# A two-layer block on one core: the second normalisation of three batches, the gate columns and the selection move

## The chip, the cores and the metric

The kernel runs on one core of a Trainium2 chip. The metric is the device time of the whole program in microseconds (us). The kernel before takes 1383.87 us, the median of three runs (1381.85 to 1384.41).

## The reference

Four batches of 512 tokens with 128 features (2048 tokens, 16 tiles of 128). Two layers, and each normalises its input and adds two results to it.

```python
xn = _layernorm(x)
x = x + _L0_attn_ref(xn, ...) + _L0_ffn_ref(xn, ...)      # 8 heads of 64; experts: 8, the best one, 80 places each
xn = _layernorm(x)
x = x + _L1_attn_ref(xn, ...) + _L1_ffn_ref(xn, ...)
# in _L1_attn_ref
q, k = xn @ Wq.T, xn @ Wk.T                               # 64 columns each
Vy = xn @ Wy_w.T + Wy_b                                   # 128 columns
e = relu(signed_sqrt(q[:, :, None, :] + k[:, None, :, :]))
scores = einsum('bija,a->bij', e, Wphi)                   # softmax over j, combined with Vy and e
# in _L1_ffn_ref
logits = xn @ gate_w + gate_b                             # 8 experts
topv, topi = top_k(logits, 2); probs = softmax(topv)      # two experts, their shares
```

## The kernel before

Four stages follow each other, each in a block of its own. A block ends for all engines together: the next one starts only when every engine has finished. Inside a block each engine runs its own list of instructions in the order written, and the lists meet at semaphores.

1. `normalise_and_route` loads the tokens into `g.x1`, normalises them into `g.xn`, transposes them into `g.xnT` and finds each token's expert, its slot and its factor `g.coef`.
2. `first_layer` is the attention of layer 0, and inside its first batch the experts of layer 0. A batch (called a row in the code) is 32 steps: 8 heads times 4 tiles of queries. In step s TensorE makes the scores of tile s, VectorE their largest value (L582), ScalarE the exponentials (L512), GpSimd divides by the sum (L462, `rescale`), TensorE transposes the result (L702), ScalarE keeps its rounded part (L525, `pT_hi`), VectorE the rest (L592, `pT_lo`), and TensorE multiplies with the values (L728 to L730). The last operations lag by up to ten steps. Once in four steps the next head's queries and keys are kept (L497, L501 on ScalarE, L564, L569 on VectorE), and in eight steps of each batch the values (L533, L607). The sum over the heads of batch b is copied, transposed and added to `g.x1` in steps 7 to 9 of batch b+1 (L612, L738, L618). After the last batch there is a drain of ten steps, in which only the lagging operations and this last addition are left. GpSimd gathers the experts' results into `g.gathered` during the second batch.
3. `second_route`, the seam between the layers. VectorE adds `g.gathered` times `g.coef` to `g.x1` tile by tile (L843, 16 instructions), takes mean and variance (L91, L94), and ScalarE the square root (L823). VectorE normalises into `xn` (L848), TensorE transposes (L894), ScalarE keeps `g.xnT` (L826). Then TensorE makes the gate logits of all 16 tiles (L901), and after them for each batch c the queries (L910), the keys (L913) and the values (L918), each into one PSUM bank; ScalarE keeps queries and keys (L831, L834), VectorE the values with their bias (L853, `keep_values`). VectorE selects the two experts of each token with `first_max` (five operations, each waiting for the one before) twice (L871, L875), ScalarE takes one exponential of the gap (L837) between batch 1 and batch 2 of its copies, and six small operations make `g.share`.
4. `second_layer` is layer 1: features, square roots and weighted sums of 32 blocks of queries, with one expert's products beside each block. It takes about 1000 of the 1381 us and is not touched by the diff.

Of the kernel before, what the change touches and what calls it, by code (L numbers as in the profile page):

```python
# [100 lines left out]
def layers_kernel(nc, x, wqk, wv, gate0_w, gate0_b, w1, b1, w2, b2,  # L101
# [7 lines left out]
    with ExitStack() as ctx:  # L109
# [25 lines left out]
        g.wq, g.wk, g.wy, g.wyb = (g.wge[:, i * P:(i + 1) * P] for i in range(4))  # L135
# [10 lines left out]
        with ExitStack() as first:  # L146
# [42 lines left out]
            g.gateb = scratch("gateb", [P, E])  # L189

# [154 lines left out]
def first_layer(nc, g, take):  # L345
# [12 lines left out]
    with ExitStack() as ctx:  # L358
# [40 lines left out]
        eo_out, gathered_in = sem("eo_out"), sem("gathered_in")  # L399
        small_in, c2_made, c2_prep = sem("small_in"), sem("c2_made"), sem("c2_prep")  # L400
# [13 lines left out]
        SCATTERS_FIRST, CONSTANTS_AT, GATHERS_AT = 3, 16, 2  # L414

# [10 lines left out]
        def _(sp):  # L426
# [5 lines left out]
            small = ((g.wq, g.a_wq), (g.wk, g.a_wk), (g.wy, g.a_wy), (g.wyb, g.a_wyb.partition_broadcast(P)),  # L432
# [11 lines left out]
        def _(pool):  # L444
# [19 lines left out]

            pool.wait_ge(zeroed, 1)
# [11 lines left out]
            pool.wait_ge(gathered_in, 16 * NT)  # L477

        @block.scalar
        def _(act):  # L480
# [22 lines left out]
            def row(b, first=False, drain=False, final=False):  # L503
                for s in range(DRAIN if drain else STEPS):
# [40 lines left out]
        def _(dve):  # L545
# [25 lines left out]

            def row(b, first=False, drain=False, final=False):
                for s in range(DRAIN if drain else STEPS):
# [29 lines left out]
                    if not drain and s - 1 in VALUES_AT:  # L603
# [4 lines left out]
                                          V_hi[:, j // 2, at].bitcast(F32), ALU.subtract).then_inc(v_kept, 1)  # L608
                    if not first and s == OUT_AT:
# [5 lines left out]
                    if not first and s == OUT_AT + 2:  # L615
                        dve.wait_ge(o_done, b)
                        xr = g.x1[:, bass.ds((b - 1) * TB, TB), :]
# [10 lines left out]
        def _(pe):  # L628
# [44 lines left out]
            def row(b, first=False, drain=False, final=False):  # L673
                for s in range(DRAIN if drain else STEPS):
# [40 lines left out]
                    for m in range(TB):  # L715
# [15 lines left out]
                        if m == TB - 1:  # L731
                            ins.then_inc(av_done, 1)
                    if not first and s == OUT_AT + 1:
# [5 lines left out]
                        ins.then_inc(o_done, 1)  # L739
                    if first:  # L740
                        experts(s)

# [43 lines left out]
def second_route(nc, g, take):  # L786


    with ExitStack() as ctx:  # L789
        def sb(name, shape, dt=F32):  # L790
            return ctx.enter_context(nc.sbuf_tensor(name, shape, dt))

# [3 lines left out]
        xn = take(NT, D)  # L796
        gw = take(E)
        p1 = take(NT)
        p2 = take(NT)
        top2 = take(NT)  # L800
        term = take(NT, E)
        psX = ctx.enter_context(nc.psum_tensor("psX1", [P, 4, 512], F32))
        psL = ctx.enter_context(nc.psum_tensor("psL1", [P, NT, E], F32))
        psP = ctx.enter_context(nc.psum_tensor("psP1", [P, 3, 512], F32))
        gate_in, r_steps = sem("gate1_in"), sem("r_steps")
        var_ready, std_ready = sem("var1_ready"), sem("std1_ready")
        xn_ready, xT_done, xT_kept = sem("xn1_ready"), sem("xT1_done"), sem("xT1_kept")
        logits_done, gap_ready, exp_done = sem("logits1_done"), sem("gap_ready"), sem("exp1_done")
# [3 lines left out]
        bias_steps = sem("bias_steps")  # L812
        block = ctx.enter_context(nc.Block())

        @block.sync
        def _(sp):
            sp.dma_start(gw, g.gate1_w).then_inc(gate_in, 16)
            sp.dma_start(g.gateb[:], g.gate1_b.partition_broadcast(P)).then_inc(gate_in, 16)

        @block.scalar  # L820
        def _(act):
            act.wait_ge(var_ready, 1)
            act.activation(g.std[:], g.std[:], ACT.Sqrt).then_inc(std_ready, 1)  # L823
            for c in range(4):
                act.wait_ge(xT_done, c + 1)
                act.activation(g.xnT[:, c * 512:(c + 1) * 512], psX[:, c, :], ACT.Copy).then_inc(xT_kept, 1)  # L826
# [13 lines left out]
        def _(dve):  # L840
            chain = Chain(dve, r_steps)
            for t in range(NT):
                chain.step(dve.scalar_tensor_tensor(g.x1[:, t, :], g.gathered[:, t, :], g.coef[:, t:t + 1],  # L843
                                                    g.x1[:, t, :], ALU.mult, ALU.add))
            chain.done()
            norm_scale(dve, chain, g.x1, g.stats, g.mv, g.std[:], g.rstd[:], var_ready, std_ready)
            for t in range(NT):
                dve.tensor_scalar(xn[:, t, :], g.x1[:, t, :], g.mv[:, t, 0:1], g.rstd[:, t:t + 1],  # L848
                                  ALU.subtract, ALU.mult).then_inc(xn_ready, 1)

            def keep_values(c):
                dve.wait_ge(v_done, c + 1)
                dve.tensor_tensor(g.V2[:, c * TB:(c + 1) * TB, 0:D], psP[:, 2, :].rearrange("p (t d) -> p t d", t=TB),  # L853
                                  g.value_bias.unsqueeze(1).to_broadcast([P, TB, D]), ALU.add).then_inc(v_kept, 1)


            dve.wait_ge(bias_done, 1)
            dve.tensor_tensor(g.value_bias, psP[:, 0, 0:D], g.web, ALU.add).then_inc(bias_steps, 1)
            dve.wait_ge(bias_steps, 1)
            dve.tensor_tensor(g.value_bias, g.value_bias, g.wyb, ALU.add).then_inc(bias_steps, 1)  # L860

# [7 lines left out]
            dve.wait_ge(logits_done, 1)  # L869
            chain.link(dve.tensor_tensor(g.lg[:], psL[:], g.gateb[:].unsqueeze(1).to_broadcast([P, NT, E]), ALU.add))  # L870
# [6 lines left out]
            keep_values(1)  # L877
# [7 lines left out]
            keep_values(2)  # L885
            keep_values(3)

        @block.tensor
        def _(pe):

# [662 lines left out]
```

## Time and profile before

| | |
|---|---|
| median of three runs | 1383.87 us |
| the profiled execution's own time | 1383.03 us |
| its span, first to last instruction | 1381.3 us |
| VectorE, TensorE, ScalarE, GpSimd busy | 88%, 88%, 82%, 64% of the span |
| last batch of the first layer with its drain | about 265 to 344.3 us |
| the seam (`second_route`) | 344.5 to 375.7 us |
| second layer | 375.7 us to the end |
| mean granted TensorE clock | 0.981 of full |

The span is from the first to the last instruction of one profiled execution; the own time has 1.7 us around it. Busy times are shares of the whole, over stages with different limits, so a stage is read by the windows and the list of instructions of its own stretch. A value in square brackets behind an instruction is the idle time of its engine ahead of it, with the instruction that ended it.

### The profile page before, as it was taken

What the parts mean: (1) busy time and instruction counts of PE and PEld (TensorE: products, weight loads), DVE (VectorE), ACT (ScalarE), POOL (GpSimd) and SP (SyncE); (2) the same over time, 40 slices, a digit from 0 to 9 for tenths busy, and PEclk for the clock granted to TensorE, in tenths of its full rate; (3) what the DMA queues carried; (4) which work ended last, traced back from release to release, by engine and by line L of the source; (5) the groups of instructions that cost most, each with busy time, mean ns of one, the idle gap of its engine ahead of it and who ended that gap; (6) DMA issues with size and microseconds to landing.
All of it is one profiled execution on the core that took longest, in us unless ns stands there. A gap on an engine that the chain in (4) does not pass through costs nothing.

```text
span 1381.3 us, 21175 instructions
## 1 busy us (share of the span) xinstructions
PE 1210.2 (88%) x6185; PEld 575.5 (42%) x6185; DVE 1212.5 (88%) x3409; ACT 1135.1 (82%) x1292; POOL 888.8 (64%) x1294
## 2 busy tenths in 40 slices
PE   3899999998659999888999989899988889998886
PEld 2577667676422333333333333333333333333333
DVE  5777989896778899999999999989999998999997
ACT  1776888886369998999999899999989999998950
POOL 0764733332007888888888788888888888888820
PEclk9999999999769999999999999999999999999998
DMA  6001100000000001000000100000000000001001
GB/s 193 9 11 24 30 1 0 0 1 1 20 0 16 20 20 28 23 27 20 20 20 20 32 23 24 20 20 20 20 31 27 20 21 20 20 21 31 28 20 35
DMA packets 38843, 32.36 MB, mean 23 GB/s; under 512 B 6150, under 2 KB 35609, under 8 KB 38738
## 3 DMA queue, kind: packets, MB, share of 16 engines
q1 hardware_dynamic: 37714, 29.76, 7.4%
q0 software_dynamic: 1024, 1.35, 0.6%
q8 instruction: 47, 0.77, 0.2%
q14 instruction: 58, 0.48, 0.1%
HBM read 29.10 MB, written 2.75 MB: 23 GB/s over the span
## 4 chain that ended last, share of the span: by engine, by line
DVE 35%; PE 32%; issue 5%; ACT 1%; POOL 0%; POOLq 0%; DVEq 0%; ACTq 0%
DVE arena L1051 21%; PE ps L1331 10%; PE ps L1344 9%; DVE arena L1037 5%; PE ps L1388 4%; PE ps L1408 4%; DVE s L1083 3%; DVE x L1094 2%; PE ps L1380 2%; PE ps L1362 2%; DVE spread L1103 2%; DVE nmax L1043 1%; PE ps L1366 1%; ACT arena L1190 1%; DVE shift L1045 0%
## 5 line engine op out<-in xcount | busy, mean ns | idle before, releaser
L1051 DVE SCALAR_TENSOR_TENSOR arena<-arena,ps 128x512 f32<-128x512 f32 x1024 | 663.8, 677 | 69.8 <-PE ps L1344 68.5
L1190 ACT ACTIVATE arena<-arena,eps 128x4096 f32<-128x4096 f32 x128 | 474.2, 3709 | 6.0 <-ACT arena L1178 5.7
L1308 POOL TENSOR_SCALAR arena<-kT,negq 128x512 f32<-128x512 f32 x480 | 344.0, 723 | 170.8 <-DVE arena L1051 161.8
L1344 PE MATMUL ps<-spread,sel 128*128 128x512 f16 x1024 | 357.9, 386 | 101.1 <-DVE arena L1051 95.0
L1314 POOL TENSOR_SCALAR arena<-arena,q 128x512 f32<-128x512 f32 x480 | 348.0, 735 | 22.4
L1344 PEld LDWEIGHTS ps<-spread,sel 128*128 128x128 f16 x1024 | 91.9, 97 | 491.5 <-DVE arena L1051 376.0
L1331 PE MATMUL ps<-arena,phi_cols 128*32 128x512 f32 x2048 | 276.3, 614 | 7.7 <-ACT arena L1190 7.7
L1178 ACT ACTIVATE arena<-kT,q 128x512 f32<-128x512 f32 x330 | 217.1, 712 | 44.3 <-DVE arena L1051 44.3
L462 POOL TENSOR_SCALAR kT<-kT,region 128x512 f32<-128x512 f32 x128 | 88.8, 694 | 155.6 <-DVE region L587 155.0
L512 ACT ACTIVATE kT<-ps,region 128x512 f32<-128x512 f32 x128 | 88.0, 687 | 59.4 <-DVE region L582 57.9
L1395 PE MATMUL ps<-z,wge 128*128 128x512 f32 x256 | 130.8, 593 | 0.3 <-DVE z L1077 0.3
L1037 DVE TENSOR_SCALAR arena<-kT,q 128x512 f32<-128x512 f32 x214 | 118.8, 577 | 0.3 <-PEq L789 0.3
L582 DVE TENSOR_REDUCE region<-ps 128x1 f32<-128x512 f32 x128 | 88.1, 689 | 24.8 <-PE ps L687 23.9
L592 DVE TENSOR_TENSOR pT_lo<-ps,pT_hi 128x512 fp32r<-128x512 f32 x128 | 86.9, 679 | 11.2 <-ACT pT_hi L525 10.9
L1331 PEld LDWEIGHTS ps<-arena,phi_cols 128*32 128x32 f32 x2048 | 41.2, 109 | 116.5 <-issue 104.0
L702 PE MATMUL ps<-ident,kT 128*128 128x128 f32 x512 | 77.4, 274 | 9.3 <-DVE pT_lo L592 9.2
L1051 DVE DVE_READ_ACCUMULATOR arena<-arena,ps 128x1 f32 x1024 | 80.2, 78 | 0.0
L702 PEld LDWEIGHTS ps<-ident,kT 128*128 128x128 f32 x512 | 61.3, 140 | 44.8 <-issue 20.1
L525 ACT ACTIVATE pT_hi<-ps 128x512 fp32r<-128x512 f32 x128 | 75.6, 590 | 2.9 <-PE ps L702 2.2
L1380 PE MATMUL ps<-xnT,w1e 128*128 128x512 f32 x128 | 68.2, 615 | 5.0 <-DVE x L1155 5.0
L1408 PEld LDWEIGHTS ps<-w3e,s 128*128 128x128 f32 x512 | 67.8, 193 | 1.6
L1388 PE MATMUL ps<-xnT,w2e 128*128 128x512 f32 x128 | 67.3, 608 | 0.3 <-DVE z L1077 0.3
(196 smaller groups left out, 1714.9 us busy)
## 6 DMA issues: line engine op xcount, KB each, us to landing
wge<-in_e_wg SPq DMA_DIRECT2D x32, 256.0 KB, 2.7
w1e<-in_e_w SPq DMA_DIRECT2D x32, 128.0 KB, 2.1
w2e<-in_e_w SPq DMA_DIRECT2D x32, 128.0 KB, 2.1
w3e<-in_e_w SPq DMA_DIRECT2D x32, 128.0 KB, 2.1
region<-in_w SPq DMA_DIRECT2D x1, 2048.0 KB
out<-x SPq DMA_DIRECT2D x4, 256.0 KB, 2.8
region<-in_wqk SPq DMA_DIRECT2D x1, 512.0 KB, 4.7
region<-in_wv SPq DMA_DIRECT2D x1, 512.0 KB, 5.4
```

Of the source, the lines that this page charges most:

```text
L702: ins = pe.transpose(ps[:, TBK[late % 2], m * P:(m + 1) * P], ex[:, late % 4, m * P:(m + 1) * P], g.ident[:])
L1037: dve.tensor_scalar(feat[:, j, QUADS * gg + c, :], kT[:, bass.ds(b * N, N)], q2[:, bass.ds(pair0 + GROUPS * c + gg, 1)], 0.0, ALU.add, ALU ...
L1051: dve.scalar_tensor_tensor(feat[:, j, k, :], feat[:, j, k, :], 1.0, psB[:, k % BANKS, :], ALU.mult, ALU.mult, accum_out=sums[:, j, gg, c:c ...
L1178: act.activation(feat[:, j, QUADS * gg + c, :], kT[:, bass.ds(b * N, N)], ACT.Relu, bias=q2[:, bass.ds(pair0 + GROUPS * c + gg, 1)]).then_ ...
L1190: act.activation(grp, grp, ACT.Sqrt, bias=eps[:]).then_inc(e_ready, 2)
L1308: pool.tensor_scalar(feat[:, j, QUADS * gg + c, :], kT[:, b * N:(b + 1) * N], HUGE, negq[:, b % 2, at - b * N // 2:at - b * N // 2 + 1], A ...
L1314: pool.tensor_scalar(f, f, 1.0, q2[:, at:at + 1], ALU.mult, ALU.add).then_inc(pool_feat, 1)
L1331: ins = pe.matmul(psS[32 * c:32 * (c + 1), :], phi_cols[:, gg, :], feat[:, j, QUADS * gg + c, :], start=(gg == 0), stop=(gg == GROUPS - 1))
L1344: pe.matmul(psB[:, k % BANKS, :], sel[:, gg, c, :], spread[:, j, :], start=True, stop=True).then_inc(bc_done, 1)
L1388: pe.matmul(psX, w2[:, f * P:(f + 1) * P], xnT[:, bass.ds(m // E * N, N)], start=True, stop=True).then_inc(right_done, 1)
L1395: ins = pe.matmul((psZ, psX)[f], wg[:, half * DFF + f * P:half * DFF + (f + 1) * P], z[:, half, :], start=(half == 0), stop=(half == 1))
L1408: ins = pe.matmul(psY[:, i * D:(i + 1) * D], s[:, f, i * P:(i + 1) * P], w3[:, f * D:(f + 1) * D], start=(f == 0), stop=(f == GT - 1))
```

## The change

- The addition of the experts' results is split. In the last batch GpSimd multiplies `g.gathered` by `g.coef` tile by tile in its first 16 steps (`scale`), and VectorE adds a batch at a time (`mix`) at the end of steps 13, 17, 21 and 25.
- In the same batch VectorE takes mean and variance of the 12 tiles of batches 0 to 2 (`statistics`, steps 19 to 31), and in the drain, after step 4, normalises them into `g.xn` (`normalise`). ScalarE takes their square root in step 3 of the drain. TensorE transposes them (`turn`) around the last output transposes in steps 7 and 8, and ScalarE copies the three results to `g.xnT` in step 9.
- In the seam only the last batch's four tiles are normalised and transposed. The gate's 8 columns stand beside the 128 value columns in one weight tile `g.wyg` (136 columns), loaded during the first layer; the separate logits matmuls are gone. Value products come first (`values`), into four banks, then queries and keys. VectorE keeps logits and values of each half batch, and the whole selection stands after all four batches are kept. ScalarE's list keeps its order: the exponential of the gap still stands behind the copies of batch 1.

```diff
+        MIX_AT = {13: 0, 17: 1, 21: 2, 25: 3}
+        STATS_AT = {19: (0, 1), 20: (2, 3), 23: (4, 5), 24: (6, 7), 27: (8, 9), 28: (10, 11)}
+        AGGR_AT = {20: (0, 1), 23: (2, 3), 24: (4, 5), 27: (6, 7), 28: (8, 9), 31: (10, 11)}
+        SOONER = NT - TB
+        ROOT_AT, NORM_AT = 3, 4
+        SOONER_BANKS = (SB[0], SB[1], PJ)
...
+                pool.tensor_scalar(g.gathered[:, t, :], g.gathered[:, t, :], 1.0, g.coef[:, t:t + 1],
+                                   ALU.mult, ALU.mult).then_inc(scaled, 1)
...
+                    if drain and s == ROOT_AT:
+                        act.wait_ge(var0_ready, 1)
+                        act.activation(g.std[:, 0:SOONER], g.std[:, 0:SOONER], ACT.Sqrt).then_inc(std0_ready, 1)
+                    if drain and s == DRAIN - 1:
+                        for c in range(B - 1):
+                            act.wait_ge(xT0_done, c + 1)
+                            act.activation(g.xnT[:, c * N:(c + 1) * N], ps[:, SOONER_BANKS[c], :],
+                                           ACT.Copy).then_inc(xT0_kept, 1)
...
+            def mix(b):
+                xr = g.x1[:, b * TB:(b + 1) * TB, :]
+                dve.wait_ge(scaled, (b + 1) * TB)
+                dve.tensor_tensor(xr, xr, g.gathered[:, b * TB:(b + 1) * TB, :], ALU.add).then_inc(mixed, 1)
...
+            def normalise():
+                dve.wait_ge(std0_ready, 1)
+                dve.reciprocal(g.rstd[:, 0:SOONER], g.std[:, 0:SOONER]).then_inc(rstd0_ready, 1)
+                dve.wait_ge(rstd0_ready, 1)
+                for t in range(SOONER):
+                    dve.tensor_scalar(g.xn[:, t, :], g.x1[:, t, :], g.mv[:, t, 0:1], g.rstd[:, t:t + 1],
+                                      ALU.subtract, ALU.mult).then_inc(xn0_ready, 1)
...
+                    if drain and s == OUT_AT:
+                        turn(0)
...
+                    if drain and s == OUT_AT + 1:
+                        turn(1)
+                        turn(2)
...
-            for t in range(NT):
-                chain.step(dve.scalar_tensor_tensor(g.x1[:, t, :], g.gathered[:, t, :], g.coef[:, t:t + 1],
-                                                    g.x1[:, t, :], ALU.mult, ALU.add))
+            for t in range(LAST, NT):
+                chain.step(dve.bn_stats(g.stats[:, t, :], g.x1[:, t, :]))
...
+                for half in range(2):
+                    t = c * TB + half * 2
+                    made = psV[:, c % 2, half, 0:2 * (D + E)].rearrange("p (t n) -> p t n", t=2)
+                    dve.tensor_tensor(g.lg[:, t:t + 2, :], made[:, :, D:D + E],
+                                      g.gate1b[:].unsqueeze(1).to_broadcast([P, 2, E]), ALU.add).then_inc(lg_made, 1)
+                    dve.tensor_tensor(g.V2[:, t:t + 2, 0:D], made[:, :, 0:D],
+                                      g.value_bias.unsqueeze(1).to_broadcast([P, 2, D]), ALU.add).then_inc(v_kept, 1)
+
+            keep_values(0)
+            keep_values(1)
...
+            keep_values(2)
+            keep_values(3)
+            dve.wait_ge(lg_made, 2 * B)
             first_max(dve, chain, g.lg[:], g.desc[:], g.top[:], g.tie[:], g.rank[:], g.mask1[:])
-            keep_values(0)
-
             chain.link(dve.scalar_tensor_tensor(g.lg[:], g.mask1[:], -1e30, g.lg[:], ALU.mult, ALU.add))
             first_max(dve, chain, g.lg[:], g.desc[:], top2, g.tie[:], g.rank[:], g.mask2[:])
             dve.tensor_tensor(p2, top2, g.top[:], ALU.subtract).then_inc(gap_ready, 1)
-            keep_values(1)
...
+            values(0)
+            values(1)
+            query(0)
+            for i in range(TB):
+                pe.wait_ge(xn_ready, i + 1)
+                ins = pe.transpose(psX[:, i * P:(i + 1) * P], xn[:, LAST + i, :], g.ident[:])
+            ins.then_inc(xT_done, 1)
+            values(2)
+            pe.wait_ge(xT_kept, 1)
+            values(3)
+            key(0)
+            for c in range(1, B):
+                query(c)
+                key(c)
```

## Rows read from the trace of the kernel before

**Rows 1.** Windows: stretch, length, each engine's busy time, granted clock, DMA.
```profile
265.00:344.50 79.50, 73.88 (x360) 53.37 (x358) 63.72 (x128) 58.77 (x131) 23.36 (x34) 1.00 0.00 1
344.50:375.70 31.20, 20.63 (x98) 14.26 (x99) 21.94 (x96) 10.69 (x20) 0.00 (x0) 0.73 0.01 1
```

**Rows 2.** Windows of four steps each in the last batch, same columns.
```profile
285.62:295.05 9.43, 9.19 (x44) 6.49 (x43) 8.52 (x18) 8.04 (x18) 2.77 (x4) 1.00 0.01 2
303.99:312.15 8.16, 7.78 (x40) 5.57 (x39) 6.88 (x14) 6.52 (x16) 2.77 (x4) 1.00 0.00 1
```

**Rows 3.** Timeline, VectorE in the last batch: start, duration, instruction, idle before.
```profile
306.28 0.69 DVE L582 TENSOR_REDUCE region<-ps 128x1 f32<-128x512 f32 x1 [0.23 <-PE ps L687]
...
307.38 0.69 DVE L592 TENSOR_TENSOR pT_lo<-ps,pT_hi 128x512 fp32r<-128x512 f32 x1 [0.34 <-ACT pT_hi L525]
...
312.15 0.69 DVE L582 TENSOR_REDUCE region<-ps 128x1 f32<-128x512 f32 x1 [0.61 <-PE ps L687]
```

**Rows 4.** Timeline, ScalarE in the same steps.
```profile
307.25 0.68 ACT L512 ACTIVATE kT<-ps,region 128x512 f32<-128x512 f32 x1
...
312.88 0.69 ACT L512 ACTIVATE kT<-ps,region 128x512 f32<-128x512 f32 x1 [0.33 <-DVE region L582]
```

**Rows 5.** Timeline of the drain.
```profile
337.70 0.60 ACT L525 ACTIVATE pT_hi<-ps 128x512 fp32r<-128x512 f32 x1 [1.23 <-PE ps L702]
...
338.33 0.69 DVE L592 TENSOR_TENSOR pT_lo<-ps,pT_hi 128x512 fp32r<-128x512 f32 x1 [1.14 <-ACT pT_hi L525]
...
342.13 0.69 DVE L612 COPY q<-ps 128x512 f32<-128x512 f32 x1 [3.11 <-PE ps L730]
...
343.57 0.69 DVE L618 TENSOR_TENSOR x<-x,ps 128x512 f32<-128x512 f32 x1 [0.75 <-PE ps L738]
```

**Rows 6.** Timeline, VectorE at the start of the seam, like instructions merged.
```profile
344.59 4.29 DVE L843 SCALAR_TENSOR_TENSOR x<-region,coef,x 128x128 f32<-128x128 f32 x16 [0.33 <-PEq L358]
348.92 3.19 DVE L91 BATCH_NORM_STATS2 stats<-x 128x6 f32<-128x128 f32 x16
352.14 1.17 DVE L94 BATCH_NORM_AGGREGATE mv<-stats 128x2 f32<-128x6 f32 x16
...
354.10 4.19 DVE L848 TENSOR_SCALAR region<-x,mv,rstd 128x128 f32<-128x128 f32 x16
```

**Rows 7.** Windows in the seam, for the granted clock (third column from the right).
```profile
362.50:365.00 2.50, 2.50 (x4) 0.96 (x4) 1.72 (x6) 0.69 (x2) 0.00 (x0) 0.50 0.00 0
...
366.00:375.60 9.60, 8.68 (x44) 5.62 (x42) 5.88 (x17) 6.03 (x12) 0.00 (x0) 1.00 0.00 0
```

**Rows 8.** Timeline, TensorE's projections in the seam; two or eight passes merged.
```profile
362.30 1.95 PE L910 MATMUL psP<-xnT,wge 128*128 128x512 f32 x2
...
371.90 1.02 PE L910 MATMUL psP<-xnT,wge 128*128 128x512 f32 x2
...
373.62 1.05 PE L918 MATMUL psP<-wge,xnT 128*128 128x128 f32 x8
```

**Rows 9.** Timeline, second half of the selection, and the table load beside it.
```profile
367.56 0.28 DVE L874 SCALAR_TENSOR_TENSOR lg<-mask,lg 128x128 f32<-128x128 f32 x1
...
369.22 1.28 ACT L837 ACT_TABLE_LOAD   x1
...
369.50 0.17 DVE L876 TENSOR_TENSOR region<-region,top 128x16 f32<-128x16 f32 x1
```

**Rows 10.** Groups of the seam on ScalarE: count, busy, mean ns, idle before.
```profile
L831 ACT ACTIVATE q<-psP 64x256 f32<-64x256 f32 x8 | 3.0, 375 | 7.0 <-PE psP L910 6.9
...
L834 ACT ACTIVATE kT<-psP 128x512 f32<-128x512 f32 x4 | 2.4, 597 | 1.1 <-PE psP L913 0.9
```

**Rows 11.** Timeline, ScalarE at a change of table in the second layer.
```profile
409.37 1.28 ACT L1190 ACT_TABLE_LOAD   x1
410.67 3.71 ACT L1190 ACTIVATE arena<-arena,eps 128x4096 f32<-128x4096 f32 x1
```

**Rows 12.** One line: ns of the shortest, median and longest, two SBUF inputs.
```profile
L1103 DVE SCALAR_TENSOR_TENSOR spread<-exh,split_by,ex x32: 740/741/1197, 414.3 to 1344.7; 128x512 f16<-128x512 f16 x32
```

More of the change, by code:

```diff
@@ L134, in layers_kernel @@
         g.value_bias = g.w1e[:, 0:D]
-        g.wq, g.wk, g.wy, g.wyb = (g.wge[:, i * P:(i + 1) * P] for i in range(4))
+        g.wq, g.wk, g.wyb = (g.wge[:, i * P:(i + 1) * P] for i in range(3))
         g.web, g.rho = g.w3e[:, 0:P], g.w3e[:, P:2 * P]
@@ L476, in _ @@
                         gather(s - GATHERS_AT)
-            pool.wait_ge(gathered_in, 16 * NT)
+                    if b == B - 1 and s < NT:
+                        scale(s)
         @block.scalar
@@ L608, in row @@
                                           V_hi[:, j // 2, at].bitcast(F32), ALU.subtract).then_inc(v_kept, 1)
+                    if final:
+                        statistics(s)
+                    if drain and s == NORM_AT:
+                        normalise()
                     if not first and s == OUT_AT:
@@ L616, in row @@
                         dve.wait_ge(o_done, b)
+                        if drain:
+                            dve.wait_ge(mixed, B)
                         xr = g.x1[:, bass.ds((b - 1) * TB, TB), :]
@@ L822, in _ @@
             act.wait_ge(var_ready, 1)
[L823 to L826, printed above, removed]
+            act.activation(g.std[:, LAST:NT], g.std[:, LAST:NT], ACT.Sqrt).then_inc(std_ready, 1)
+            act.wait_ge(xT_done, 1)
+            act.activation(g.xnT[:, LAST * P:NT * P], psX[:], ACT.Copy).then_inc(xT_kept, 1)
             qv = psP[:, 0, :].rearrange("p (n h) -> p n h", h=2)
@@ L847, in _ @@
-            for t in range(NT):
+            for t in range(LAST, NT):
+                chain.step(dve.bn_aggr(g.mv[:, t, :], g.stats[:, t, :]))
+            chain.done()
+            dve.tensor_scalar(g.std[:, LAST:NT], g.mv[:, LAST:NT, 1], LN_EPS, None, ALU.add).then_inc(var_ready, 1)
+            dve.wait_ge(bias_done, 1)
+            dve.tensor_tensor(g.value_bias, psP[:, 0, 0:D], g.web, ALU.add).then_inc(bias_steps, 1)
+            dve.wait_ge(std_ready, 1)
+            chain.link(dve.reciprocal(g.rstd[:, LAST:NT], g.std[:, LAST:NT]))
@@ L848, in _ @@
+            for t in range(LAST, NT):
                 dve.tensor_scalar(xn[:, t, :], g.x1[:, t, :], g.mv[:, t, 0:1], g.rstd[:, t:t + 1],
                                   ALU.subtract, ALU.mult).then_inc(xn_ready, 1)
+            dve.wait_ge(bias_steps, 1)
+            dve.tensor_tensor(g.value_bias, g.value_bias, g.wyb, ALU.add).then_inc(bias_steps, 1)
             def keep_values(c):
                 dve.wait_ge(v_done, c + 1)
[L853 to L854 removed]
@@ L884, in _, with values, query @@
             dve.tensor_tensor(g.share[:], term, g.mask2[:], ALU.add)
[L885 to L886 removed]
         @block.tensor
         def _(pe):
[L891 to L905 removed]
+            def values(c):
+                if c >= 2:
+                    pe.wait_ge(v_kept, 2 * (c - 1))
+                    pe.wait_ge(lg_made, 2 * (c - 1))
+                for i in range(TB):
+                    t = c * TB + i
+                    ins = pe.matmul(psV[:, c % 2, i // 2, i % 2 * (D + E):(i % 2 + 1) * (D + E)],
+                                    g.xnT[:, t * P:(t + 1) * P], g.wyg[:], start=True, stop=True)
+                ins.then_inc(v_done, 1)
+            def query(c):
                 if c:
```

96 lines of the change are left out of this document (49 added, 47 removed).

## The prediction

> **What bounds the kernel now.** I read the windows first, because the busy shares of the whole say little: VectorE is at 88% over three stages with different limits. The change touches the last batch with its drain and the seam [rows 1]. The second layer starts when the block of the seam has ended for all engines, so every microsecond of the seam counts once; in the seam VectorE is busy for 21.94 of 31.20 us and TensorE for 20.63, one after the other, and the granted clock averages 0.73. The reader should see a serial chain there. The timeline gives its pieces: VectorE alone until 354.1 (mixing 4.29, statistics 3.19 and 1.17, small ones 0.7) while TensorE has nothing to do; then normalising, 4.19 [rows 6]; then the logits and, from 362.30, the projections to 375.4 [rows 8].
>
> The last batch is different. Four steps take 8.16 us, with VectorE at 6.88, ScalarE at 6.52 and TensorE at 7.78 busy [rows 2]. Nobody is full; the three wait for each other in turn, and what VectorE has spare is three small gaps, 0.23, 0.34 and 0.61 us [rows 3].
>
> **The last batch.** VectorE gets 4 mixes, 12 statistics, 12 aggregations and one addition. Like instructions follow each other every 0.20 us (3.19/16) and 0.073 us (1.17/16) [rows 6]; a 128x512 addition lasts 0.69 [rows 5] and takes about 0.60 of the engine, since neighbours overlap by 0.08. That is 2.40 + 2.40 + 0.88 + 0.15 = 5.8 us of work. How much becomes time?
>
> A mix stands behind the kept query, at a place where 0.23 us are idle [rows 3], so it pushes the next maximum by 0.4. That exponential starts at 307.25 with no idle time ahead of it [rows 4]: ScalarE had been busy, and the maximum had ended at 306.97. So the exponential moves by 0.2 and the rest part at 307.38, which waits for ScalarE, not at all. I take 0 for a mix. The nearest measured row is the output addition of the same size at the same place in step 9: its four steps took 9.43 against 8.16 [rows 2], but these also hold two parts of the values and four transposes on TensorE. It is the upper bound.
>
> Two statistics behind step 19 and two with two aggregations behind step 20 put 0.40 + 0.55 us into a stretch that ends in the 0.61 gap at 312.15 [rows 3]. About 0.3 stays over, and there the exponential does wait for the maximum [rows 4], so it is passed on. Three such pairs of steps: 0.9. The last two aggregations and the addition behind step 31 fall ahead of a wait for ScalarE; 0.1 to 0.3. Sum for the batch: +1.2. Bounds: 0, everything in the gaps, and +5.8, nothing.
>
> GpSimd gets 16 scales of 128x128. Its busy time is 2.77 in four steps of 8.16 [rows 2]; a scale is shorter than one of its 0.69 rescales, which are four times as wide, and fits behind each. I take 0; 0 to 0.7 as bounds. Should these scales be late, the mix of step 13 waits for the four of steps 0 to 3, far behind.
>
> **The drain.** Before, ScalarE ends at 338.30, VectorE at 339.02, then VectorE waits 3.11 us for the last product, copies at 342.13 and adds at 343.57, end 344.26 [rows 5]. Into these 3.11 us goes the normalising, but it has to wait for a root. The root's table is not loaded, since the batch uses the exponential: a load of 1.28 and a root that starts right behind it [rows 11], 0.21 for the root. 338.31 + 1.28 + 0.22 = 339.8. Reciprocal 0.25 and its wait, then 12 tiles at 0.262 (4.19/16) [rows 6]: 340.1 + 3.15 = 343.3. The copy comes at 343.3 in place of 342.13, so the addition ends at 345.4. Behind the four output transposes TensorE has eight more, each 0.12 to 0.16 at full clock: 345.8. ScalarE, which copies the three transposed batches last in its list, copies the first at 342.8 and the others at 345.3 and 345.85, 0.60 each, and ends at 346.45. New late one: ScalarE's third copy. The drain grows by 346.45 − 344.26 = 2.2. Bounds: 1.1, if the copies hide (VectorE's end alone), and 3.4, if the clock is at half and the eight transposes take twice as long.
>
> The Trainium skill (*ScalarE: Activation LUTs*, "What ACT_TABLE_LOAD costs") puts a switch at about 2.66 us, load and drain together, against the 1.28 + 0.02 of the row above. By that the root would come 1.4 later, and the sum would be 1.4 worse; the trace disagrees, and the sum goes by the trace.
>
> **The seam, counted from its start.** Gone: the mixing (4.29), three quarters of statistics (2.39 + 0.88) and of normalising (3.14), 12 transposes and 3 copies, and the separate logits, 3.8 us of TensorE. The eight columns beside 128 cost 8/128 of the value products, 0.06 us a batch.
>
> VectorE: 4 statistics 0.80, 4 aggregations 0.30, addition 0.18 and waits: 1.45. Bias 0.28 beside the root; reciprocal and four tiles 2.0 to 3.1; second bias 3.4. TensorE starts values at 0.5 without waiting. After the idle end of the drain I take it at half clock for four to five microseconds: the same projection ran at 0.50 and 1.95 us at 362.5, and at 1.00 and 1.02 us from 366 on [rows 7, 8]. Values of one batch: 0.95 at full (1.05 less overlap [rows 8], plus the columns), 1.9 at half. So values(0) 2.4, values(1) 4.3, first query 5.6, transposes 6.1, values(2) 7.0, values(3) 8.0, first key 8.9. ScalarE's copy of the last transposes is at 6.75, ahead of values(3).
>
> VectorE keeps a batch in about 1.0 (four instructions, between the 0.17 and the 0.69 of their widths): batches 0 and 1 by 5.5, constants 6.1, batches 2 and 3 by 9.15. Now the selection, all behind it. Its second half, from the masking to the gap, is 367.56 to 369.67 = 2.1 [rows 9], the first half five of its steps = 1.6: gap at 12.9. Here the change adds a wait that was not one before: ScalarE's exponential stands behind the copies of batch 1, which end at 11.2. It waits till 12.9, and behind it are queued the query and key copies of batches 2 and 3, and for these TensorE waits, because there is one bank for queries and one for keys. The table load of 1.28 lies in this wait, as it ran ahead of the gap before [rows 9]. From there: exponential 13.15, query copy 0.78 (two of 0.375 and a start [rows 10]), query(3) 1.02 (a copy releases it at 13.95), its copy 15.8, and key copy 0.60: 16.45. VectorE's six small ones end at 14.8. With 0.28 to the next block: 16.7 against 31.14 (344.56 to 375.70), a gain of 14.4. If the clock is full from the start, TensorE is 2 us earlier, VectorE only 0.7: 15.0. Bounds of the seam: 12 to 16.
>
> **The second layer.** The same instructions start earlier, from the same state; its first 40 us go through stretches at either clock, so I allow ±1.5 and take 0.
>
> Sum: +1.2 + 2.2 − 14.4 = −11.0. Against the profiled execution's own 1383.03 that is 1372.0; the median of the runs is 0.84 above that execution, which gives 1372.9. I forecast 1372.5.
>
> The Trainium skill (*SBUF — State Buffer*, "SBUF: two separate sides") says that a VectorE instruction with two SBUF inputs and a GpSimd instruction that reads SBUF exclude each other for their whole length. The mix has two SBUF inputs, and GpSimd rescales all through the batch. Four collisions at 0.69 would make the sum −8.2. The trace shows such a VectorE instruction at 741 ns in the median and 1197 at the longest of 32, with GpSimd busy beside it [rows 12]: a wait exists but is rare.
>
> **Rivals.**
> 1. The batch pays in full, +5.8. For: the loop has no full engine but is a ring of waits, and the additions of step 9 came with longer steps. Against: the gaps [rows 3]. Time 1372.5 + 4.6 = 1377.
> 2. TensorE stays at half clock through the seam. For: projections did run at half for 3.5 us [rows 7] right after the clock had been full. Against: from 366 the same mix ran at full. Then values(3) end at 10.8, gap at 15.6; TensorE's pairs take 1.74 in place of 0.86, and queries and keys of the last two batches stand behind the exponential: end about 23.5, seam gain 7.2. Time 1380.
> 3. Slower than before: the two engines' new instructions exclude each other in the last batch. Place: 16 scales and 4 mixes against maxima, rest parts and rescales there. Price: one full wait of 0.69 for each of the 20, 13.8, on top of 5.8; sum 19.6 + 2.2 − 14.4 = +7.4, 1390. It decides from 12.2 us of growth of the batch. Against it: rows 12, and GpSimd's free 66%.
> 4. The selection hides after all, for ScalarE gets its gap before the copies of batch 1 are done. Then TensorE's pairs bound the seam: 8.0 + 7 × 0.86 + copy 0.7 = 14.7, gain 16.1: 1371. Against: it would need the gap 1.7 us sooner.
> 5. The seam saves, but something gives it all back in the second layer, whose tiles are long (unchanged period): no change, 1383.
>
> **Chances.** Forecast, 1369.5 to 1375.5: 0.68. Rival 1: 0.13. Rival 2: 0.07. Rival 3: 0.02. Rival 4: 0.06. Rival 5: 0.04. A measurement of this kernel tells some 0.2%, 2.8 us, from no change. Faster by over 0.2% are the forecast, rivals 1, 2 and 4: 0.94; within: 0.04; slower: 0.02. The range leaves out rivals 2, 3 and 5 and the thin ends: 1369.3 to 1378.
>
> **What would show it.** The last batch's steps 17 to 29 take 24.5 us before; 25.4 would be right, 28 rival 1. In the drain: a table load at once behind the last rounded part, VectorE's copy near 1.2 us later than the last product, ScalarE's third copy as the last instruction. In the seam: 16.5 us, ScalarE's exponential after an idle of about 0.4 to 1.7 us that VectorE's gap ended, and a TensorE gap ahead of query(3). If instead the seam ends soon after VectorE's keeping, the placing of that wait is wrong; if TensorE's clock is at 0.50 past its fifth microsecond, rival 2 is at work. The forecast is wrong above all if the second layer's start is not 9 to 13 us earlier.

## The result and the profile after

The changed kernel takes 1366.05 us (median of three, 1365.13 to 1366.76) against 1383.87: 0.9882 of before, 95% interval 0.9858 to 0.9905, so 17.8 us faster. The forecast was 1372.5 with a range of 1369.3 to 1378. The direction was right, the forecast gain of 11 us too small, and the time lies outside the range. In a second comparison, that of the run `after_again`, the ratio was 0.9845 (0.9823 to 0.9867).

The profiled execution took 1366.76 us, span 1365.0. Read by stages, the pair of profiles gives this:

| stage | before | after | difference | forecast |
|---|---|---|---|---|
| copy of step 7 to last maximum of the last batch | 49.44 | 49.96 | +0.5 | +1.2 |
| last maximum to the seam's first instruction | 12.24 | 14.11 | +1.9 | +2.2 |
| seam | 31.14 | 14.99 | −16.1 | −14.4 |
| start of the second layer to its first spread | 38.52 | 36.90 | −1.6 | 0 ± 1.5 |
| rest of the second layer | 967.05 | 966.42 | −0.6 | 0 |

With 0.3 us from ahead of step 7 that is −16.3, the two spans.

First the last batch after the change, windows of four steps (columns as in [rows 1]). They answer to [rows 2]:

```profile
303.65:311.93 8.28, 7.88 (x41) 5.56 (x40) 8.16 (x21) 6.39 (x15) 2.78 (x4) 1.00 0.00 1
...
311.93:320.34 8.41, 7.96 (x41) 5.49 (x39) 8.29 (x24) 6.83 (x16) 2.79 (x4) 1.00 0.01 2
```

VectorE is now busy for 8.29 of 8.41 us, where it had 6.88 of 8.16; 1.3 to 1.4 us of work a group became 0.12 to 0.25 us of time. From the maximum of step 17 to that of step 29 it is 25.11 us, before 24.49; the prediction named 25.4 as the sign of its being right and 28 as that of rival 1. One scale on GpSimd takes 0.37 us behind a rescale, with 0.8 to 1.6 us idle ahead of the next rescale.

The drain, from the timeline (start, duration, instruction, idle before), answers to [rows 5]:

```profile
338.55 1.28 ACT L550 ACT_TABLE_LOAD   x1
...
339.84 0.21 ACT L550 ACTIVATE std<-std 128x12 f32<-128x12 f32 x1
...
340.35 3.17 DVE L624 TENSOR_SCALAR region<-x,mv,rstd 128x128 f32<-128x128 f32 x12
...
343.43 0.68 DVE L671 COPY q<-ps 128x512 f32<-128x512 f32 x1
...
344.66 1.04 PE L816 MATMUL ps<-ident,region 128*128 128x128 f32 x8
...
345.30 1.08 ACT L554 ACTIVATE xnT<-ps 128x512 f32<-128x512 f32 x2 [1.90 <-PE ps L816]
```

Each of these instructions starts within 0.25 us of where the forecast put it. The reader should see the root 0.01 us behind its table load: the 2.66 us for a switch that the Trainium skill gives (*ScalarE: Activation LUTs*, "What ACT_TABLE_LOAD costs") are not seen here either.

The seam is one window, all of it at full clock; it answers to the second row of [rows 1], where the mean clock was 0.73:

```profile
346.69:361.67 14.98, 12.48 (x54) 7.12 (x55) 11.83 (x55) 7.49 (x16) 0.00 (x0) 1.00 0.00 1
```

And its end, ScalarE, TensorE and VectorE, answers to [rows 8, 9]:

```profile
356.50 1.28 ACT L905 ACT_TABLE_LOAD   x1
...
357.60 0.17 DVE L955 TENSOR_TENSOR rstd<-region,top 128x16 f32<-128x16 f32 x1
357.81 0.22 ACT L905 ACTIVATE rstd<-rstd 128x16 f32<-128x16 f32 x1
...
358.75 1.12 PE L981 MATMUL psP<-xnT,wge 128*128 128x512 f32 x2 [1.00 <-ACT q L899]
...
360.76 0.60 ACT L902 ACTIVATE kT<-psP 128x512 f32<-128x512 f32 x1
```

The gap (the difference of the two best logits, L955) is ready at 357.77 and the table at 357.78. The queue behind this exponential is as forecast: TensorE waits 1.00 us for the query bank, and the last key copy ends the seam.

### The profile page after: what moved, and what is told of

It reads as the page before. It is cut to its first block, busy times and chain, and to the rows that moved or that the text cites. A ratio compares the mean times of both kernels' runs of the same rounds, so it can differ in the third digit from the quotient of the medians.

```text
span 1365.0 us, 21144 instructions
## 1 busy us (share of the span) xinstructions
PE 1200.5 (88%) x6153; PEld 568.3 (42%) x6153; DVE 1210.0 (89%) x3410; ACT 1135.8 (83%) x1293; POOL 895.9 (66%) x1310
## 4 chain that ended last, share of the span: by engine, by line
DVE 35%; PE 32%; issue 6%; ACT 1%; POOL 0%; POOLq 0%; DVEq 0%; ACTq 0%
DVE arena L1133 22%; PE ps L1413 10%; PE ps L1426 9%; DVE arena L1119 5%; PE ps L1470 4%; PE ps L1490 4%; DVE s L1165 3%; DVE x L1176 2%; PE ps L1462 2%; PE ps L1444 2%; DVE spread L1185 2%; DVE nmax L1125 1%; PE ps L1448 1%; ACT arena L1272 1%; PE ps L1477 0%
```

## The experiments

Stage lengths are read from each run's profile, since the whole varies between executions by more than some of the effects (the kernel before lay between 1379 and 1387 us in all but one of its executions).

**The same kernels again.** What belongs to a kernel, and what to an execution?

> The kernel before, once more, for one profile. From the start of the second layer's block to its first spread it took 39.97 us less 1.45, that is 38.5 (375.73 to 414.25), against 36.9 (361.68 to 398.58) in the changed kernel, and in the changed one TensorE's clock rose earlier there. Theory: the gain in the second layer follows from the change, since TensorE enters it differently; then this profile shows 38.5 again, within 0.3. Rival: where the clock falls and rises there depends on the execution alone; then this profile may lie anywhere from 36.9 to 38.5, and nothing of it is the change's.

> The changed kernel once more, with its time against the kernel before on the same chip. 17 us faster, 1366. Theory (the entry decides): block start to first spread 36.9 again, within 0.3. Rival (each execution has its own): up to 38.5. The seam is 15.0 us in both, since its TensorE work ran at the full clock all through.

> The kernel before, once more for its profile. Theory: in its seam the clock rises at no fixed instruction, and the seam's length follows it: 31.1 to 31.2 us where the clock is full for the logits (as in the first profile), 34.8 where it stays at half through them (as in the second); so the base that I forecast from was the lucky one of two. This one: 31 to 35, and its length follows the time at which the clock rises. Rival: 31.1 is the rule and 34.8 an exception that the median doesn't hold: 31.0 to 31.3.

> The same, a fourth profile. Theory: seam between 31 and 35 us, again following the clock. Rival: 31.0 to 31.3.

| execution | seam | layer start to first spread | rest | time |
|---|---|---|---|---|
| before | 31.14 | 38.52 | 967.05 | 1383.03 |
| before_again | 34.82 | 37.85 | 965.49 | 1384.85 |
| before_third | 35.13 | 37.69 | 965.66 | 1382.03 |
| before_fourth | 32.47 | 37.69 | 965.61 | 1379.04 |
| after | 14.99 | 36.90 | 966.42 | 1366.76 |
| after_again | 14.99 | 38.46 | 967.05 | 1369.23 |

The seam of the kernel before has no fixed length. Its 32 passes of logits show why; the timelines of before_again and of before_fourth:

```profile
358.97 6.83 PE L901 MATMUL psL<-region,xnT 128*128 128x8 f32 x32
...
365.66 2.05 PE L910 MATMUL psP<-xnT,wge 128*128 128x512 f32 x2
```

```profile
355.41 4.27 PE L901 MATMUL psL<-region,xnT 128*128 128x8 f32 x32
...
359.54 2.05 PE L910 MATMUL psP<-xnT,wge 128*128 128x512 f32 x2
```

6.83 us (in before_third too) for what took 3.83 in the profile I forecast from. In before_again the granted clock stayed at 0.50 through all of it:

```profile
361.00:363.00 2.00, 2.00 (x11) 2.00 (x11) 0.00 (x0) 0.00 (x0) 0.00 (x0) 0.50 0.00 0
```

In the profile I forecast from, the clock was full for most of the logits and fell behind them, with TensorE busy throughout (the logits last from 358.6 to 362.4; from 362.5 the clock is at 0.50 [rows 7]):

```profile
360.00:362.00 2.00, 2.00 (x20) 2.00 (x20) 0.00 (x0) 0.00 (x0) 0.00 (x0) 1.00 0.00 0
```

The four seams average 33.4 us, mine was the shortest. Measured against this mean the seam gains 18.4, not 16.1; it is a mean of four executions that differ by 4 us. The start of the second layer is the other way round: after_again took 38.46, as long as any of before, so the 1.6 us there belonged to that execution. My theory that the entry decides is refuted; the rival holds.

The whole time varies for one more reason, which the traces show though no run was made for it. The first stage also makes gate logits, 32 passes of 8 columns. The timelines of before and of before_fourth:

```profile
17.00 6.83 PE L336 MATMUL psL<-gw,xnT 128*128 128x8 f32 x32
```

```profile
16.91 3.74 PE L336 MATMUL psL<-gw,xnT 128*128 128x8 f32 x32
```

They take 6.83 us in 12 of the 16 profiles, and 3.7 to 4.2 in the other four: before_third, before_fourth, move_only and narrow_logits. These four are also the ones that reach the copy of step 7 at 279.6 to 280.1 us, where all others reach it at 282.5 to 283.2. In the four, the granted clock fell about 20 us after the start, in the last part of these passes. In the other twelve the clock column reads 1.00 in this stage, but a pass takes 0.21 us, as at 0.50 in the seam of before_again; there the duration tells, not the column. The pair before and after both had the long one, so their difference of 16.3 us holds nothing of it.

**The two halves of the change, each alone.** `seam_only` leaves the first layer as it was and has only the new order and the joined gate columns; `move_only` has only the moved work, and its seam makes logits, then query, key and value products batch by batch. Both are shown against the changed kernel, shortened:

```diff
 # seam_only: nothing in the last batch or drain; in the seam, for all 16 tiles
-                    if b == B - 1 and s < NT:
-                        scale(s)
...
-                    if final:
-                        statistics(s)
-                    if drain and s == NORM_AT:
-                        normalise()
...
+            for t in range(NT):
+                chain.step(dve.scalar_tensor_tensor(g.x1[:, t, :], g.gathered[:, t, :], g.coef[:, t:t + 1],
+                                                    g.x1[:, t, :], ALU.mult, ALU.add))
...
+            for t in range(NT):
+                if t in (2 * TB, 3 * TB):
+                    pe.wait_ge(xT_kept, t // TB - 1)
+                pe.wait_ge(xn_ready, t + 1)
+                ins = pe.transpose(psX[:, t // TB % 2, (t % TB) * P:(t % TB + 1) * P], xn[:, t, :], g.ident[:])
...
 # move_only: the seam's TensorE list in the old order
+            for t in range(NT):
+                ins = pe.matmul(psL[:, t, :], g.xnT[:, t * P:(t + 1) * P], g.wyg[:, D:D + E], start=True, stop=True)
+            ins.then_inc(logits_done, 1)
+            for c in range(B):
+                xc = g.xnT[:, c * N:(c + 1) * N]
...
```

> Only the second half of the change: nothing is moved into the first layer; in the seam all 16 tiles are mixed, normalised and transposed first, and then come the joined value products, queries, keys and the selection in the new order. Theory: front of the seam as before, 13.8 us to the last normalised tile, then the rest about as long as in the changed kernel, with TensorE at half clock in the first microseconds: seam 27 to 28 us against 31.1, so 3 to 4 us faster than before (1380). Rival, the order and the joined columns carry the larger part of the seam's gain: 24 us, 7 faster.

> Only the first half: mixing, statistics, normalising and transposing of three batches stand in the last batch and the drain as in the changed kernel; the seam makes its logits with separate matmuls and its projections and selection in the old order. Theory: the last batch and drain cost 2.4 us as in the changed kernel; the seam is transposes at about 3.5, logits 1.9 to 3.8, and projections as before 11 to 13: 18 to 19 us; total 10 to 11 us faster than before (1373). Rival (the order carries the larger part): the seam stays at 22 us or more, 7 us faster.

Measured: seam_only 1378.07 us, 0.9956 of before (0.9938 to 0.9975), seam 28.40. move_only 1376.47, 0.9939 (0.9918 to 0.9959), seam 23.49, not the 18 to 19 I expected. The first is near the expectation. The second missed by 5 us: its seam is where the rival had it (22 us or more), and its time is 8.4 us below the 1384.89 of before, between the 10 to 11 of the theory and the 7 of the rival. Its windows show where the 5 us are:

```profile
343.80:347.00 3.20, 1.24 (x6) 0.73 (x7) 2.98 (x16) 0.20 (x1) 0.00 (x0) 1.00 0.01 3
347.00:349.00 2.00, 2.00 (x14) 2.00 (x13) 0.69 (x6) 0.60 (x1) 0.00 (x0) 0.66 0.00 0
349.00:351.00 2.00, 2.00 (x11) 2.00 (x11) 0.00 (x0) 0.00 (x0) 0.00 (x0) 0.50 0.00 0
...
355.00:357.00 2.00, 2.00 (x4) 0.74 (x3) 0.44 (x2) 0.76 (x2) 0.00 (x0) 0.50 0.00 0
```

The seam starts at full clock. The clock falls at about 347.6, 0.5 us after the logits (matmuls of 8 columns) have begun, and stays at half through them and the first projections, about 10 us, with TensorE busy all the time. Ahead of the logits TensorE had been busy for only 1.24 of 3.20 us, so this run alone leaves two causes for the fall, the idle time and the narrow matmuls. Against the mean seam of 33.4 the halves gain 5.0 and 9.9, together 14.9; both at once gain 18.4.

**Is it the narrow matmuls, or the idle time ahead?** Three kernels on the changed one:

```diff
 # narrow_logits (12 matmuls of 8 columns) and wide_logits (12 of 128), results unused
+            for t in range(LAST):
+                pe.matmul(psL[:, t * E:(t + 1) * E], g.xnT[:, t * P:(t + 1) * P], g.wyg[:, D:D + E], start=True, stop=True)
             values(0)
 # the same matmul in wide_logits
+                pe.matmul(psL[:, t % 4 * D:(t % 4 + 1) * D], g.xnT[:, t * P:(t + 1) * P], g.wyg[:, 0:D], start=True, stop=True)
 # cold_entry: VectorE at the end of the drain
+                            for n in range(8):
+                                dve.tensor_copy(oT, ps[:, AV, :]).then_inc(idled, 1)
+                                dve.wait_ge(idled, n + 1)
```

> The changed kernel with 12 of the old 16 logits matmuls (8 columns wide) made again at the start of the seam; their results are not used, so nothing else changes. By themselves they are 24 passes at 0.12 us, 2.9 us. Theory N (in the part that only moved the work, the clock was full at the seam's start and fell at 347.7 while TensorE issued just these matmuls, and stayed at half for 10 us): the clock falls here too, the seam grows from 15.0 to 20 us or more, above all its queries, keys and values at 1.9 us a pair. Rival (idle time ahead of the seam decides, and there is little here): the clock stays full and the seam is 17.9 us.

> The same with the 12 extra matmuls 128 columns wide instead of 8, results unused too. By themselves 12 times 0.24 to 0.26, some 3.0 us. Theory N: wide ones keep the clock full, seam 18.0 us, no more, so some 3 us faster than with narrow ones though each matmul does 16 times the columns. Rival (any extra TensorE work ahead costs what it takes, the clock follows idle time alone): the same 17.9 to 18.2 us in both.

> The changed kernel with eight extra copies on VectorE, one after another, at the end of the drain (about 5.8 us), so that TensorE has nothing to do for some 6 us ahead of the seam. Theory I (idle time ahead lets the clock fall): the seam starts at half clock, and is 16 to 18 us in place of 15.0; the whole is 5 us slower by the copies and 1 to 3 by the clock. Rival (only the narrow matmuls do it): seam 15.0, whole 5 us slower.

| kernel | seam | clock in it |
|---|---|---|
| after | 14.99 | 1.00 all through |
| wide_logits | 16.86 | 1.00 all through |
| narrow_logits | 20.16 | 0.50 from about 1.2 us after its start, for 6.8 us |
| cold_entry | 16.20 | 0.50 for the first 4.2 us |

One window of narrow_logits and one of wide_logits:

```profile
345.00:351.00 6.00, 6.00 (x29) 6.00 (x29) 2.12 (x10) 0.21 (x1) 0.00 (x0) 0.50 0.01 1
```

```profile
346.90:363.80 16.90, 14.94 (x79) 9.84 (x80) 12.10 (x56) 7.48 (x16) 0.02 (x1) 1.00 0.00 0
```

The reader should compare TensorE's busy time: all of the window in the first, and the clock at half none the less. The same number of matmuls, 16 times as wide, costs 1.87 us (1.1 less than I expected, for I had taken all of their 3.0 us as added); the narrow ones cost 5.17. TensorE's idle time ahead of the seam is the same 1.0 us in both. Idle time ahead lowers the clock too, but the 6 us of cold_entry cost 1.2. Both causes exist; in these sizes the narrow matmuls are the larger.

Each of these seams is that of one profile, and the whole times do not confirm the 3.3 us between the first two: 1368.06 (1367.71 to 1370.50) for narrow_logits, 1369.07 (1365.95 to 1371.44) for wide_logits, with the ratio 0.988 for both; cold_entry has 1371.21. The profiled execution of narrow_logits was one with the short logits of the first stage, which gave it 3.2 us; of its other three there is no profile.

Beside this pair it speaks for the narrow matmuls that the clock fell in the midst of such passes or right behind them, with TensorE busy all the time, in the seams of before, before_fourth and before_warm and in the first stage of four executions.

**The kernel before with TensorE kept busy.**

```diff
+            for _ in range(10):
+                pe.matmul(psP[:, 1, :], g.wq, g.xnT[:, 0:N], start=True, stop=True)
             for t in range(NT):
                 pe.wait_ge(xn_ready, t + 1)
```

> The kernel before with ten extra 128x512 matmuls on TensorE at the start of its seam, results unused, while VectorE mixes and normalises (8.6 us at full clock, in 9.4 us that are idle). Theory: the seam of the kernel before is long partly because its TensorE work runs at half clock; but the 16 narrow logits matmuls let the clock fall again, as they did in the two runs with them, so it gains little: seam 29 to 31 us against 31.1 and 34.8 in the two profiles. Rival (idle time ahead is the cause of the half clock): all TensorE work at full, seam 27.5 us (31.14 less 1.9 for the first queries and keys, 1.1 for transposes and values and 0.6), and no more spread between executions.

Seam 30.82, ratio 1.0008 (0.9991 to 1.0024). The seam is shorter than all four of before, by 2.6 us against their mean, but the whole time shows no gain, and its interval leaves room for 1.2 us at most; so the mean of 33.4 may be too high, or something was lost elsewhere. As the theory had it: the clock was full through transposes and logits, and fell behind the logits, for the first projections. This seam window shows it:

```profile
360.00:362.00 2.00, 2.00 (x20) 2.00 (x19) 0.00 (x0) 0.00 (x0) 0.00 (x0) 1.00 0.00 0
...
364.00:366.00 2.00, 2.00 (x6) 1.15 (x5) 0.34 (x2) 1.05 (x3) 0.00 (x0) 0.50 0.00 0
```

**What the last batch pays.** The 16 scales, 4 mixes, 12 statistics and 12 aggregations are left out of it.

> The changed kernel with the 16 scales on GpSimd, the 4 mixes, 12 statistics and 12 aggregations left out of the last batch (the experts' results are not added, and the old means are used). It measures what they cost there: from the copy in step 7 to the last maximum the kernel before took 49.44 us and the changed one 49.96. Theory: 49.44 again, so 28 VectorE instructions, 5.8 us of work, cost 0.5. Rival: the last batch varies by itself by more than that (49.2 or 49.8).

From the copy of step 7 to the last maximum: 49.46, against 49.94 to 50.00 with them in nine executions. Six more executions without them (the kernel before four times, before_warm and seam_only) took 49.43 to 49.53. So 5.8 us of VectorE work cost 0.5 us; the rival (variation) is out.

**Three versions beyond the change.** `both_tables` puts the exponential behind batch 2 and loads both tables early; `layer_warm` fills TensorE's idle time at the start of the second layer; the last has both.

```diff
 # both_tables
-                if c == 1:
+                if c == 2:
                     act.wait_ge(gap_ready, 1)
+            act.activation(g.warm[:], g.eps[:], ACT.Exp)      # behind the seam's root
+                act.activation(warm2[:], eps[:], ACT.Sqrt)    # first in the second layer
 # layer_warm
+                        pe.matmul(ps[:, 2, :], ident[:], xnT[:, 0:N], start=True, stop=True)   # 6, 3 x 1, 4, 3 times
```

> The changed kernel with its exponential of the gap behind the copies of batch 2 instead of batch 1, its table loaded by a one-column exponential right behind the seam's root, while ScalarE is idle, and the root's table loaded the same way at the start of the second layer. Theory (the wait for the gap, and the load in it, set the seam's end; and the load of 1.28 stands ahead of the first roots): seam 13.7 to 14.0 against 14.99, layer start to first spread 1.3 less; 2.3 to 2.6 us faster than the changed kernel. Rival (TensorE's pairs bound the seam): seam 14.8 or more, 1.3 us faster in all.

> The changed kernel with 16 extra matmuls in the idle stretches of TensorE at the start of the second layer, results unused (six ahead of the first scores, one behind each second group, four ahead of the first products, three behind them). Theory: the 36.2 to 38.5 us from the start of the layer to the first spread vary with the clock there; at full clock the first maximum comes at 23.0 to 23.5 and the spread at 36, and the first tile runs at full: 1.5 to 4 us faster than the changed kernel, and less spread. Rival (VectorE's and ScalarE's chain bounds that stretch, the clock only moves TensorE inside it): within 1 us of the changed kernel.

> Both of the last two together, a version meant to beat the changed kernel. Theory: the gains add, 4 to 6 us faster than the changed kernel (1360 to 1362). Rival (the stretch is bound by VectorE, so the gains overlap): 2.5 us.

both_tables: 1364.30 us, 0.9881 of before (0.9855 to 0.9908), seam 13.99. The seam gained 1.0 us, the least of what the theory had. The first roots start 3.67 us after the layer's start, in place of 4.94, but the spread came at 36.54, 0.4 below the changed kernel's 36.90 and above the 36.20 of no_statistics, whose second layer is the changed kernel's own. So of the 1.3 us nothing is shown to reach the spread. TensorE's last four pairs now start 0.96 to 1.04 us apart, against 0.86 in the seam of before, and the last two query copies wait some 0.45 for their pairs. The rival had this as a bound at 14.8; it lies at or below 13.99.

layer_warm: 1367.35, 0.9894 (0.9865 to 0.9924), first spread at 39.52, later than in any other execution. Both the theory (1.5 to 4 us faster than the changed kernel) and the first-spread time of 36 missed. Its clock shows a second place, the products with the second bias (8 rows deep, 381.04 to 385.4):

```profile
381.00:383.00 2.00, 2.00 (x18) 1.96 (x18) 0.05 (x1) 1.96 (x2) 0.00 (x0) 1.00 0.00 0
383.00:385.00 2.00, 2.00 (x16) 2.00 (x16) 0.00 (x0) 0.00 (x0) 0.00 (x0) 0.79 0.00 0
385.00:387.00 2.00, 2.00 (x10) 0.53 (x13) 0.00 (x0) 0.00 (x0) 0.00 (x0) 0.50 0.00 0
```

TensorE had been busy without a gap since 378.1 and at full clock; the clock fell at about 384.2, among these products, and the last scores took 3.64 us in place of 2.65 in the profile after, with the first maximum waiting for them. In tables_and_warm it fell at 382.9, right behind them. That their shape is the cause is not tested: no run made them wider. One of my extra matmuls also stood ahead of them. tables_and_warm: 1365.31, 0.9875 (0.9852 to 0.9898), no better than both_tables, and not the 4 to 6 us expected. Of the three, none is told apart from the changed kernel by its whole time; both_tables has a seam 1.0 us shorter.

## Why the prediction was wrong

**The reading of what bounds it: right.** A serial seam, with VectorE first and TensorE after, and a last batch with gaps in it.

**The last batch, +1.2: right in kind, too high.** 0.5 measured. The mix that stands alone, in step 13, was free, as argued (8.94 us for its four steps in both); the three pairs of steps with statistics passed on 0.12 to 0.25 each, the other mixes included, not 0.3. Rival 1 would have been 5.8.

**The drain, +2.2: right.** 1.87. ScalarE's third copy is the last, as named.

**The failed step is the seam, in both of its terms of clock.** The new seam was put at 16.7 with "After the idle end of the drain I take it at half clock for four to five microseconds". It ran at full clock throughout, and VectorE kept a batch in 0.84 us, not 1.0: 14.98 to 15.00 in the four executions with this seam (after, after_again, layer_warm, no_statistics). The prediction had 15.0 for a full clock, so with that choice the new seam is right to 0.1. Rival 4 had a seam of the same length for another reason, a gap that comes early; that is not what happened, since ScalarE's exponential did wait. cold_entry shows what a half clock at the start would have cost, 1.2 us. The old seam, the 31.14 that is subtracted from, was the shortest of four: 31.14 to 35.13, mean 33.4. I had the row that said so, projections at 0.50 right behind a stretch at full clock [rows 7], and used it only for rival 2, as a danger for the new seam. What lay between the two was the logits, and the change takes these away. So the joined columns are worth more than the 3.8 us of passes that I counted: 12 of the 16 narrow matmuls alone, put back in narrow_logits, made the seam 5.2 us longer. That narrow matmuls are the cause is shown by the seams of narrow_logits and wide_logits, one profile of each. Together the seam's two terms are −18.4 measured for −14.4 forecast.

**The second layer, 0 ± 1.5.** −1.6 and −0.6 in the pair of profiles; the repeats put both within one kernel's variation. In the means of four profiles before and two after the stages give +0.5 + 1.9 − 18.4 = −16.0, the layer's start −0.3 (37.9 and 37.7) and the rest +0.8 (966.0 and 966.7): −15.5. So the profile I forecast from was short in its seam by 2.3 us and long behind it by 1.7; as a whole it was a fair base, and the pair's own −16.3 comes out near the means for that reason. −15.5 agrees with the first comparison (−13.1 to −19.7) and not with the second (−18.4 to −24.5). What the second had on top is open. The logits of the first stage, 3 us shorter in some executions of any kernel, can shift a comparison so; which of its executions had them is not shown, for only two of that comparison's executions of the two kernels were profiled.

**The waits.** The exponential's wait was named as the seam's end; it was, though at 0.03 us behind its own table load, so load and gap ended together. By the Trainium skill (*SBUF — State Buffer*, "SBUF: two separate sides") a VectorE instruction with two SBUF inputs and a GpSimd instruction that reads SBUF exclude each other. The mixes did not put this to the test: they lasted 692 to 695 ns, and GpSimd ran nothing during any of the four. One of them, between two rescales:

```profile
304.51 0.69 POOL L475 TENSOR_SCALAR kT<-kT,region 128x512 f32<-128x512 f32 x1 [1.20 <-DVE region L642]
307.20 0.70 POOL L475 TENSOR_SCALAR kT<-kT,region 128x512 f32<-128x512 f32 x1 [2.00 <-DVE region L642]
...
305.74 0.69 DVE L603 TENSOR_TENSOR x<-x,region 128x512 f32<-128x512 f32 x1
```

So rival 3 had no place to act. In the second layer they do meet, and there the trace goes the way of the Trainium skill: of GpSimd's instructions that write `arena` from `kT` and `negq`, the 30 that start during VectorE's instruction of [rows 12] last 1005 ns in the median, the other 450 last 688. So there GpSimd pays, which the prediction did not see: it read VectorE's 741 ns alone and called the wait rare.

**The range** did not take in the bounds of my terms: added up at their low ends they give 0 + 1.1 − 16 − 1.5 = −16.4, that is 1367.5, and the range began at 1369.3. The measured 1366.05 lies below both; the base, a single execution, had no bound at all.

## What to carry to other kernels

Take a stage that is to be shortened from several profiles before subtracting from it, if its clock column is not constant: the length of the base can vary by more than the terms in dispute. Where a clock falls while TensorE is busy, look at how narrow its matmuls are; here 8 columns joined to a product of 128 cost almost nothing (16 passes of 136 took 2.12 us, 8 of 128 took 1.05) and took away a stretch at half clock that a count of passes doesn't show. Small instructions go nearly free into a ring of waits, if each lands in a gap: 5.8 us for 0.5.

## What the hardware showed that I had not expected

- The granted clock fell from full to half with TensorE busy without a gap, in or right behind matmuls of 8 columns: at 362.4 us in before, 358.2 in before_fourth, 362.9 in before_warm and about 20 us after the start in four executions. In narrow_logits it fell at 344.9, 0.8 us after such matmuls had begun; with 128 columns in the same place (wide_logits) it stayed at 1.00. It also fell in or right behind products 8 rows deep (384.2 in layer_warm, 382.9 in tables_and_warm).
- The same 32 passes of 128x8 took 3.83, 4.27, 6.83 and 6.83 us in the seams of four executions of one kernel, and 3.7 to 6.8 us in the first stage, which alone moves the whole time by 3 us.
- Six microseconds of idle TensorE ahead of the seam cost 1.2 us in it, less than the 12 narrow matmuls' 5.2.
- In the second layer GpSimd's instructions that start during VectorE's instruction of [rows 12], which has two SBUF inputs, last 1005 ns in place of 688 (medians of the profile before).
